# Half a piece in each tick, in place of a whole piece in every other one, for chains that stand alone

## The chip, the cores and the metric

The kernel runs on one core of one Trainium2 chip. Its time is the device time in microseconds (us), the median of several runs; a profiled execution of the same program gives the trace.

## The reference

Two layers of cross attention, with x of shape (4, 1024, 512) and ctx of the same shape, all in fp32:

```python
def layer0(q, k, v):                       # 16 heads of 32
    Q, K, V = (heads(a @ W.T + b) for ...) # from x, ctx, ctx
    att = softmax(Q @ K.T / sqrt(32))
    x = (att @ V) @ Wo.T + bo + q
    return layernorm(x) * gamma + beta

def layer1(query, key, value):             # linear attention, no heads
    KV = einsum('bnd,bne->bde', elu(key), value)
    Z = 1 / (elu(query) . elu(key).sum(1) + 1e-6)
    x = query + (elu(query) @ KV) * Z
    return layernorm(x) * gamma + beta

x = layer0(x, ctx, ctx); x = layer1(x, ctx, ctx)
```

(`heads` and `layernorm` stand for what the reference writes out. The kernel works with elu(x) as the larger of x and exp(min(x, 0)) - 1.)

## The kernel before, in words

The work of layer 0 is cut into 64 units: 4 batches x 4 groups of 4 heads x 4 chunks of 256 queries. A unit has 16 half steps, so there are HALVES = 1024 of them, and the whole kernel is one loop over **ticks** k, from -14 to some 1,098, which every engine's program goes through in the same order. In tick k TensorE does, in this order:

- `pass1(k)`, line 471: one score matmul in two-term precision (512 keys for 128 queries of one head), into one of three banks `score`. VectorE takes its maximum (line 810).
- `pass2(k - 26)`, line 485: two matmuls of 256 columns into one of two banks `scoreT`, the maxima included. ScalarE takes the exponential into a ring `p_ring` of 7 places (line 657); GpSimd adds pairs of the ring (lines 1072, 1081), VectorE the other half of the sums (line 850), for the softmax's denominators.
- `beside(k)`: one **piece** of a chain, if the planner put one at this tick (`pieces[k]`).
- in every eighth tick (39, 47, 55, ...) a **visit**, lines 503 and 519: the product of four ring places with V. A tick with a visit never has a piece.

The **chains** are all other work of TensorE, and each accumulates in one of two banks `misc`, taken by turns. K (4 pieces of one fp32 matmul of 512 columns; line 542), V (4 pieces of 4 fp32 matmuls of 128 columns; 553) and Q (2 pieces of 2 matmuls of 256 columns; 529) are projections; O (4 pieces of 512 columns; 565) is the output projection of a tile of 128 rows; T (573) turns a tile's features, and A (4 pieces; 582) multiplies them with the key-value sum of layer 1; S (8 pieces of 512 columns; 590) makes that sum from features that ScalarE (746, 749) and VectorE (990) make some ticks ahead and GpSimd sums up (1123, 1127); N totals the features; B folds a bias. An fp32 matmul is two instructions on TensorE, each with a weight load of its own; fp32r matmuls (score, scoreT, A) are one.

When a chain's last piece has ended, ScalarE and VectorE take the result out of the bank in the same tick, by `ended`, and the next chain but one waits for that in `chain_freed`. `follow` then books the steps behind it: transfers on SP's queue by `send`, norms on ScalarE, VectorE and GpSimd by `book`, each at the first tick with room.

The planner walks through the ticks. At each tick without a visit it takes, of the chains that are ready, the one whose due time (`deadline`) comes first, and lays its pieces into the ticks that follow. A chain is **alone** by this test:

```python
alone = len(able) == 1 and 0 <= k < HALVES and (k < UT * UB or k % (UT * UB) >= 180) and deadline(*chain) - k > 2 * LENGTH[chain[0]] + 4
```

UT * UB is 256, the ticks of a batch. A chain that is alone has its pieces in every other tick: after each piece (`k - 1 in pieces`) one tick stays free. All other chains have theirs in tick after tick.

`sum_piece(k)` tells ScalarE, VectorE and GpSimd which feature to make for the S piece at tick k; they ask for it with k + 4, k + 3 and k + 2. The ring `fphi_sb` has 3 places; VectorE waits in `context_features` for `T["kv_piece"]` of the piece three before.

The tail: after tick 1023 there are no more scores, after tick 1049 no second passes, and the last batch's eight tiles go through O, norm, T, A and the last norm.

Of the kernel before, what the change touches and what calls it, by code (L numbers as in the profile page):

```python
# [12 lines left out]
def build(nc, x, xT, ctx, ctxT, WqT, WkT, WvT, cols, WoT, bo, gamma0, beta0, gamma1, beta1, out):  # L13
    B, S, D = x.shape
    P = nc.NUM_PARTITIONS
# [58 lines left out]
    with ExitStack() as c:  # L74
# [122 lines left out]

        LENGTH = {"K": 4, "V": 4, "Q": 2, "O": 4, "T": 1, "A": 4, "S": 8, "N": 1, "B": 4}  # L200
        TILE_TICKS = 21

# [124 lines left out]
        def follow(kind, i):  # L327
# [28 lines left out]
            if kind == "S":  # L356
                if i % G == G - 1 and i < G * (B - 1):
                    for t in range(0, KT, 2):
                        send("ctx", end + 2 + t, KT * (i // G + 1) + t, 2)
                for k in range(start_of["S", i], end + 1):  # L360
                    if k in pieces and pieces[k][0] == ("S", i):
                        take("ACT", k - 4, 5)
                        take("DVE", k - 3, 5)
                        take("POOL", k - 2, 5)
            elif kind == "O":
                k = finish_norm(i, 0, end)
                k = book("below", "ACT", max(k + 2, dot_of.get(i - 2, FIRST) + 1), 7, i)
# [15 lines left out]
        while waiting:  # L383
# [34 lines left out]
        LAST = max(store_of.values()) + 2  # L418
        assert all(tiles == sorted(tiles) for tiles in
# [16 lines left out]
        def bank_of(kind, i):  # L436
            return misc[number[kind, i] % 2]
# [10 lines left out]

        def sum_piece(k):

            chain, piece = pieces.get(k, (None, 0))
            return KT * chain[1] + piece if chain and chain[0] == "S" else None


        def tensor_program():
# [68 lines left out]
            def q_project(unit, piece):  # L524
                if piece == 0:
# [5 lines left out]
                if piece == 1:  # L531
                    mm.then_inc(T["q_projected"], 1)

            def k_project(i, t):
                group, h = divmod(i, 2)
                if t == 0:
                    pe.wait_ge(M["wk"], landed(group, 1, 1))
                if i == 0:
                    pe.wait_ge(M[f"ctxT_block{t}"], 16)
                elif t == 0 and (h > 0 or group >= G):  # L540
# [5 lines left out]
            def v_project(i, t):  # L546
                group, h = divmod(i, 2)
                if t == 0:
# [6 lines left out]
                if t == G - 1:  # L555
                    mm.then_inc(T["v_projected"], 1)

            def o_project(tile, g):
                b, t = divmod(tile, KT)
                unit = unit_at[G * b + g, t // TPC]  # L560
                if g == 0:
# [3 lines left out]
                mm = pe.matmul(bank_of("O", tile)[:], outT[:, unit % NO, t % TPC * P:(t % TPC + 1) * P], wo[:, g, :],  # L565
                               start=g == 0, stop=g == G - 1)
                if g == G - 1:
                    mm.then_inc(T["o_projected"], 1)

            def turn_phi(tile):  # L570
# [13 lines left out]
                if d == G - 1:  # L584
                    mm.then_inc(T["attended"], 1)

            def sum_kv(i, t):
                piece = KT * i + t
                pe.wait_ge(V["f_phi"], piece + 1)
                pe.matmul(bank_of("S", i)[:], fphi_sb[:, piece % NPHI, :], ctx_nat[:, t, :],  # L590
                          start=t == 0, stop=t == KT - 1).then_inc(T["kv_piece"], 1)

            def total(b):
                pe.wait_ge(L["totalled"], G * (KT - 1) * (b + 1))
# [9 lines left out]
                    mm.then_inc(T["bias_passed"], 1)  # L604

            def beside(k):
                chain, piece = pieces.get(k, (None, 0))
                if not chain:
                    return
                kind, i = chain  # L610
                if piece == 0 and chain_freed(kind, i):
                    pe.wait_ge(*chain_freed(kind, i))
                if kind == "Q":
                    q_project(i, piece)
                elif kind == "K":
                    k_project(i, piece)
                elif kind == "V":
                    v_project(i, piece)
                elif kind == "O":
                    o_project(i, piece)  # L620
                elif kind == "T":
                    turn_phi(i)
                elif kind == "A":
                    attend(i, piece)
                elif kind == "S":
                    sum_kv(i, piece)
# [723 lines left out]
```

## Time and profile before

| what | us |
|---|---|
| median of 3 runs | 1512.66 (1512.58 to 1513.71) |
| span of the profiled execution | 1509.6 |
| own time of the profiled execution | not given apart from its span |
| TensorE busy | 1473.3 |
| VectorE busy | 1227.3 |
| GpSimd busy | 1206.0 |
| ScalarE busy | 900.9 |
| TensorE weight loads busy | 1038.6 |

The span runs from the first instruction to the last; a run's time holds what lies around it too. PE is TensorE, PEld its weight loads, DVE VectorE, ACT ScalarE, POOL GpSimd, SP SyncE. A matmul's recorded duration takes in the pipeline, so the sums of PE overlap; the time that one takes of the engine is seen in the distance from start to start. A matmul's record can begin while the one before it still streams.

### The profile page before, as it was taken

What the parts mean: (1) busy time and instruction counts of PE and PEld (TensorE: products, weight loads), DVE (VectorE), ACT (ScalarE), POOL (GpSimd) and SP (SyncE); (2) the same over time, 40 slices, a digit from 0 to 9 for tenths busy, and PEclk for the clock granted to TensorE, in tenths of its full rate; (3) what the DMA queues carried; (4) which work ended last, traced back from release to release, by engine and by line L of the source; (5) the groups of instructions that cost most, each with busy time, mean ns of one, the idle gap of its engine ahead of it and who ended that gap; (6) DMA issues with size and microseconds to landing.
All of it is one profiled execution on the core that took longest, in us unless ns stands there. A gap on an engine that the chain in (4) does not pass through costs nothing.

```text
span 1509.6 us, 30353 instructions
## 1 busy us (share of the span) xinstructions
PE 1473.3 (98%) x10584; PEld 1038.6 (69%) x10584; DVE 1227.3 (81%) x2442; ACT 900.9 (60%) x1846; POOL 1206.0 (80%) x1031
## 2 busy tenths in 40 slices
PE   8999999999999999999999999999999999999996
PEld 6767767676766767667677767766767767766554
DVE  6687898878788788887779788898688978899865
ACT  3464655556666666665566665665566666566664
POOL 0487787867898898877789988887789888888964
PEclk9999999999999999999999999999999999999999
DMA  7745163443425225344343425424252442520001
GB/s 222 200 144 143 54 181 128 130 128 97 122 73 157 89 90 146 105 132 138 90 129 98 135 68 158 149 87 133 79 157 77 129 127 70 148 88 26 14 23 42
DMA packets 159575, 170.14 MB, mean 113 GB/s; under 512 B 20288, under 2 KB 122048, under 8 KB 159424
## 3 DMA queue, kind: packets, MB, share of 16 engines
q1 hardware_dynamic: 157696, 167.16, 37.4%
q8 instruction: 84, 1.38, 0.4%
q10 hardware_dynamic: 1728, 1.05, 0.2%
q14 instruction: 67, 0.55, 0.1%
HBM read 125.97 MB, written 42.21 MB: 111 GB/s over the span
## 4 chain that ended last, share of the span: by engine, by line
PE 85%; DVE 4%; DMA 3%; issue 3%; POOL 2%; ACT 2%; SPq 1%; POOLq 0%; ACTq 0%; DVEq 0%
PE score L471 15%; PE scoreT L485 14%; PE acc L503 14%; PE misc L565 7%; PE misc L542 7%; PE misc L553 7%; PE misc L590 7%; PE misc L529 6%; PE misc L582 5%; PE acc L519 2%; DVE maxes L810 1%; POOL pair_sum L1072 1%; DMA q_stack<-q_dram 1%; PE misc L573 1%; DVE pair_sum L850 1%
## 5 line engine op out<-in xcount | busy, mean ns | idle before, releaser
L657 ACT ACTIVATE p_ring<-scoreT 128x512 f32<-128x512 f32 x1024 | 594.2, 594 | 496.9 <-PE scoreT L485 493.6
L1072 POOL TENSOR_TENSOR pair_sum<-p_ring 128x512 f32<-128x512 f32 x504 | 665.5, 1329 | 173.9 <-ACT p_ring L657 111.5
L810 DVE TENSOR_REDUCE maxes<-score 128x1 f32<-128x512 f32 x1024 | 677.3, 679 | 151.2 <-PE score L471 146.0
L471 PE MATMUL score<-k_stack,q_stack 96*128 96x512 f32 x1024 | 599.5, 587 | 5.4 <-DVE maxes L810 2.1
L485 PEld LDWEIGHTS scoreT<-q_stack,k_stack 104*128 104x128 f32 x2048 | 387.7, 191 | 156.7 <-ACT p_ring L657 81.6
L485 PE MATMUL scoreT<-q_stack,k_stack 104*128 104x256 f32 x2048 | 419.7, 287 | 7.3 <-ACT p_ring L657 5.1
L471 PEld LDWEIGHTS score<-k_stack,q_stack 96*128 96x128 f32 x1024 | 193.1, 189 | 161.5 <-issue 106.6
L503 PE MATMUL acc<-p_ring,v_sb 128*32 128x256 f32 x4096 | 249.9, 385 | 0.0
L1081 POOL TENSOR_TENSOR pair_sum<-pair_sum 128x512 f32<-128x512 f32 x189 | 248.8, 1316 | 0.0
L850 DVE TENSOR_TENSOR pair_sum<-pair_sum 128x512 f32<-128x512 f32 x189 | 197.2, 1043 | 1.9 <-POOL pair_sum L1072 1.7
L503 PEld LDWEIGHTS acc<-p_ring,v_sb 128*32 128x32 f32 x4096 | 120.6, 110 | 85.3 <-issue 3.2
L553 PE MATMUL misc<-wv,ctxT_sb 128*128 128x128 f32 x1024 | 134.6, 274 | 0.0
L565 PE MATMUL misc<-wo,outT 128*128 128x512 f32 x256 | 131.1, 599 | 3.4 <-DVE ctxT_sb L966 2.7
L542 PE MATMUL misc<-ctxT_sb,wk 128*128 128x512 f32 x256 | 131.1, 596 | 1.6 <-DMA ctxT_sb<-ctxT_in 1.6
L590 PE MATMUL misc<-ctx_nat,fphi_sb 128*128 128x512 f32 x256 | 132.0, 596 | 0.5 <-DVE fphi_sb L990 0.5
L529 PE MATMUL misc<-xT_sb,wq 128*128 128x256 f32 x512 | 131.6, 379 | 0.2 <-DVE k_low L903 0.2
L553 PEld LDWEIGHTS misc<-wv,ctxT_sb 128*128 128x128 f32 x1024 | 126.0, 191 | 0.8 <-issue 0.5
L1101 POOL TENSOR_TENSOR tiles<-tiles,gamma_row 128x512 f32<-128x512 f32 x52 | 72.2, 1389 | 34.8 <-ACT tiles L693 34.7
L529 PEld LDWEIGHTS misc<-xT_sb,wq 128*128 128x128 f32 x512 | 88.4, 189 | 8.6 <-issue 0.7
L990 DVE SCALAR_TENSOR_TENSOR fphi_sb<-f_sb,ctx_nat 128x128 f32<-128x128 f32 x128 | 81.7, 638 | 1.6 <-ACT f_sb L749 1.3
L1093 POOL TENSOR_TENSOR rstd<-var_eps,minus_half 128x1 f32<-128x1 f32 x64 | 40.3, 630 | 40.9 <-ACT var_eps L704 40.5
L1127 POOL TENSOR_TENSOR phi_total<-phi_total,fphi_sb 128x128 f32<-128x128 f32 x96 | 54.4, 567 | 23.1 <-DVE fphi_sb L990 22.8
(112 smaller groups left out, 1373.9 us busy)
## 6 DMA issues: line engine op xcount, KB each, us to landing
xT_sb<-xT_in SPq DMA_DIRECT2D x63, 512.0 KB, 3.8
q_stack<-q_dram SPq DMA_DIRECT2D x189, 128.0 KB, 2.6
k_stack<-k_dram SPq DMA_DIRECT2D x93, 256.0 KB, 4.7
ctx_nat<-ctx_in SPq DMA_DIRECT2D x32, 256.0 KB, 4.7
q_dram<-q_high SPq DMA_DIRECT2D x63, 128.0 KB, 1.9
q_dram<-q_low SPq DMA_DIRECT2D x63, 128.0 KB, 2.1
k_dram<-k_high SPq DMA_DIRECT2D x31, 256.0 KB, 2.0
k_dram<-k_low SPq DMA_DIRECT2D x31, 256.0 KB, 2.2
```

Source lines behind the costliest of these rows:

```text
L471: pe.matmul(score[k % 3][:], q_stack[0:SPLIT, unit % NQ, j, t * P:(t + 1) * P], k_stack[0:SPLIT, group_of[unit] % 2 * QUAD + j, h * HALF:( ...
L485: mm = pe.matmul(scoreT[k % 2][:, (j % 2) * CH:(j % 2 + 1) * CH], k_stack[0:ROWS, group_of[unit] % 2 * QUAD + j, kt * P:(kt + 1) * P], q_s ...
L503: mm = pe.matmul(acc[j * DK:(j + 1) * DK, 0:CH], v_sb[:, group % 2, kt, j * DK:(j + 1) * DK], p_ring[:, n % NP, j * CH:(j + 1) * CH], star ...
L529: mm = pe.matmul(bank_of("Q", unit)[:, 0:CH], wq[:, t, :], xT_sb[:, unit % 2, t, :], start=t == 0, stop=t == G - 1)
L542: mm = pe.matmul(bank_of("K", i)[:], wk[:, t, :], ctxT_sb[:, h, t, :], start=t == 0, stop=t == G - 1)
L553: mm = pe.matmul(bank_of("V", i)[:, t * P:(t + 1) * P], ctxT_sb[:, h, f, t * P:(t + 1) * P], wv[:, f, :], start=f == 0, stop=f == G - 1)
L565: mm = pe.matmul(bank_of("O", tile)[:], outT[:, unit % NO, t % TPC * P:(t % TPC + 1) * P], wo[:, g, :], start=g == 0, stop=g == G - 1)
L590: pe.matmul(bank_of("S", i)[:], fphi_sb[:, piece % NPHI, :], ctx_nat[:, t, :], start=t == 0, stop=t == KT - 1).then_inc(T["kv_piece"], 1)
L657: act.activation(p_ring[:, n % NP, h * HALF:(h + 1) * HALF], scoreT[k % 2][:], ACT.Exp, scale=SCALE).then_inc(A["exped"], 1)
L810: dve.reduce_max(maxes[:, unit % 2, t, j, h:h + 1], score[k % 3][:], AX.X).then_inc(V["maxed"], 1)
L1072: pool.tensor_tensor(pair_sum[:, place_of_pair(pair), cols], p_ring[:, (n - 1) % NP, cols], p_ring[:, n % NP, cols], ALU.add).then_inc(L[" ...
L1081: pool.tensor_tensor(whole, whole, part, ALU.add).then_inc(L["run_low"], 1)
```

## The change

Chains of the kinds K, V, Q, O and S that are alone are now `halved`: each piece is two parts, FIRST_PART and SECOND_PART, in the next two ticks that have no visit, with no tick left free after them. K, O and S pieces are halved by columns (`columns_of`: 256 of 512 for each part, with the same weights loaded for both), V and Q pieces by source blocks (`steps_of`: the same matmuls, the first half of them in the first part). Waits at a chain's or a piece's start are in the first part, increments in the second. Of the chains that are alone, only others (A, T, N, B) keep the free ticks. A feature of an S piece is made and booked by its first part's tick.

```diff
+        WHOLE, FIRST_PART, SECOND_PART = range(3)
...
-                    if k in pieces and pieces[k][0] == ("S", i):
+                    if k in pieces and pieces[k][0] == ("S", i) and pieces[k][2] != SECOND_PART:
                         take("ACT", k - 4, 5)
                         take("DVE", k - 3, 5)
                         take("POOL", k - 2, 5)
...
+            halved = alone and chain[0] in "KVQOS"
             for piece in range(LENGTH[chain[0]]):
-                if alone and k - 1 in pieces:
+                if alone and not halved and k - 1 in pieces:
                     k += 1
-                while visiting(k) is not None:
+                for part in (FIRST_PART, SECOND_PART) if halved else (WHOLE,):
+                    while visiting(k) is not None:
+                        k += 1
+                    pieces[k] = chain, piece, part
+                    end_of[chain] = k
                     k += 1
-                pieces[k] = chain, piece
-                end_of[chain] = k
-                k += 1
...
-            chain, piece = pieces.get(k, (None, 0))
-            return KT * chain[1] + piece if chain and chain[0] == "S" else None
+            chain, piece, part = pieces.get(k, (None, 0, WHOLE))
+            return KT * chain[1] + piece if chain and chain[0] == "S" and part != SECOND_PART else None
+
+        def columns_of(part):
+
+            return {WHOLE: slice(0, HALF), FIRST_PART: slice(0, HALF // 2), SECOND_PART: slice(HALF // 2, HALF)}[part]
+
+        def steps_of(part, first, count):
+
+            middle = first + count // 2
+            return {WHOLE: range(first, first + count), FIRST_PART: range(first, middle),
+                    SECOND_PART: range(middle, first + count)}[part]
...
-                for t in range(2 * piece, 2 * piece + 2):
+                for t in steps_of(part, 2 * piece, 2):
...
-                mm = pe.matmul(bank_of("K", i)[:], wk[:, t, :], ctxT_sb[:, h, t, :], start=t == 0, stop=t == G - 1)
-                if t == G - 1:
+                mm = pe.matmul(bank_of("K", i)[:, columns_of(part)], wk[:, t, :], ctxT_sb[:, h, t, columns_of(part)],
+                               start=t == 0 and part != SECOND_PART,
+                               stop=t == G - 1, skip_group_check=True)
+                if t == G - 1 and part != FIRST_PART:
                     mm.then_inc(T["k_projected"], 1)
...
-                for f in range(G):
+                for f in steps_of(part, 0, G):
...
-                pe.wait_ge(V["f_phi"], piece + 1)
-                pe.matmul(bank_of("S", i)[:], fphi_sb[:, piece % NPHI, :], ctx_nat[:, t, :],
-                          start=t == 0, stop=t == KT - 1).then_inc(T["kv_piece"], 1)
+                if part != SECOND_PART:
+                    pe.wait_ge(V["f_phi"], piece + 1)
+                mm = pe.matmul(bank_of("S", i)[:, columns_of(part)], fphi_sb[:, piece % NPHI, :],
+                               ctx_nat[:, t, columns_of(part)], start=t == 0 and part != SECOND_PART,
+                               stop=t == KT - 1, skip_group_check=True)
+                if part != FIRST_PART:
+                    mm.then_inc(T["kv_piece"], 1)
```

O pieces are changed as K's are, and all functions take the part as one more argument.

## Rows read from the trace of the kernel before

**Rows 1.** The page, parts 1, 2 and 5: busy us (share of the span), instructions; slices; groups.

```profile
PE 1473.3 (98%) x10584; PEld 1038.6 (69%) x10584; DVE 1227.3 (81%) x2442; ACT 900.9 (60%) x1846; POOL 1206.0 (80%) x1031
...
PE   8999999999999999999999999999999999999996
...
PEclk9999999999999999999999999999999999999999
...
L1072 POOL TENSOR_TENSOR pair_sum<-p_ring 128x512 f32<-128x512 f32 x504 | 665.5, 1329 | 173.9 <-ACT p_ring L657 111.5
L810 DVE TENSOR_REDUCE maxes<-score 128x1 f32<-128x512 f32 x1024 | 677.3, 679 | 151.2 <-PE score L471 146.0
```

**Rows 2.** Timeline of TensorE around 75 us: start, us, what, xcount [idle before].

```profile
75.17 0.40 PE L471 MATMUL score<-k_stack,q_stack 96*128 96x512 f32 x1
...
75.64 0.39 PE L471 MATMUL score<-k_stack,q_stack 96*128 96x512 f32 x1
77.64 0.51 PE L485 MATMUL scoreT<-q_stack,k_stack 104*128 104x256 f32 x2 [1.61 <-ACT p_ring L657]
77.98 0.39 PE L471 MATMUL score<-k_stack,q_stack 96*128 96x512 f32 x1
...
80.94 0.63 PE L471 MATMUL score<-k_stack,q_stack 96*128 96x512 f32 x1
```

**Rows 3.** Timeline of TensorE, 206 to 213 us: K pieces, then Q pieces, in consecutive ticks.

```profile
206.54 0.79 PE L471 MATMUL score<-k_stack,q_stack 96*128 96x512 f32 x1
...
207.87 0.80 PE L471 MATMUL score<-k_stack,q_stack 96*128 96x512 f32 x1
...
210.75 0.59 PE L471 MATMUL score<-k_stack,q_stack 96*128 96x512 f32 x1
...
212.09 0.58 PE L471 MATMUL score<-k_stack,q_stack 96*128 96x512 f32 x1
```

**Rows 4.** Timeline of TensorE, 115 to 118 us: a K chain with empty ticks between.

```profile
115.66 0.40 PE L471 MATMUL score<-k_stack,q_stack 96*128 96x512 f32 x1
...
116.13 1.02 PE L542 MATMUL misc<-ctxT_sb,wk 128*128 128x512 f32 x2
116.59 0.80 PE L471 MATMUL score<-k_stack,q_stack 96*128 96x512 f32 x1
...
117.46 0.40 PE L471 MATMUL score<-k_stack,q_stack 96*128 96x512 f32 x1
...
118.39 0.80 PE L471 MATMUL score<-k_stack,q_stack 96*128 96x512 f32 x1
```

**Rows 5.** Timeline of TensorE at 37 us, before the second pass begins.

```profile
37.13 0.50 PE L471 MATMUL score<-k_stack,q_stack 96*128 96x512 f32 x1 [0.18 <-DVE maxes L810]
```

**Rows 6.** Windows of core 0: PE, PEld, DVE, ACT, POOL busy (x), PEclk, DMA share, GB/s.

```profile
77.98:82.34 4.36, 4.36 (x15) 2.83 (x14) 3.94 (x12) 2.99 (x9) 3.28 (x4) 0.61 0.42 135
344.80:348.20 3.40, 3.36 (x22) 1.96 (x24) 3.25 (x5) 1.53 (x3) 3.40 (x4) 0.50 0.31 99
1339.00:1360.00 21.00, 20.46 (x142) 12.97 (x142) 21.00 (x37) 13.37 (x33) 20.77 (x20) 1.00 0.16 47
1460.00:1510.00 50.00, 36.05 (x242) 22.95 (x240) 24.19 (x63) 25.63 (x57) 20.96 (x21) 0.95 0.09 32
```

**Rows 7.** Window of line 590 alone (S 5): PE and PEld busy (x), PEclk, DMA share.

```profile
612.60:633.00 20.40, 8.22 (x16) 2.46 (x16) 1.00 0.19 60
```

**Rows 8.** Timeline of TensorE: V pieces in a row, V piece alone, Q piece alone.

```profile
47.23 0.48 PE L471 MATMUL score<-k_stack,q_stack 96*128 96x512 f32 x1
...
48.61 0.48 PE L471 MATMUL score<-k_stack,q_stack 96*128 96x512 f32 x1
...
55.31 0.40 PE L471 MATMUL score<-k_stack,q_stack 96*128 96x512 f32 x1
...
57.16 0.40 PE L471 MATMUL score<-k_stack,q_stack 96*128 96x512 f32 x1
...
67.23 0.40 PE L471 MATMUL score<-k_stack,q_stack 96*128 96x512 f32 x1
...
69.05 0.40 PE L471 MATMUL score<-k_stack,q_stack 96*128 96x512 f32 x1
```

More of the change, by code:

```diff
@@ L522, in visit, with q_project, k_project @@
                 mm.then_inc(T["divided"], 1)
-            def q_project(unit, piece):
-                if piece == 0:
+            def q_project(unit, piece, part):
+                if piece == 0 and part != SECOND_PART:
                     pe.wait_ge(M["wq"], 16 * (wq_load_of[unit] + 1))
                     pe.wait_ge(M[f"xT{unit % 2}"], landed(unit, 2, 1))
-                for t in range(2 * piece, 2 * piece + 2):
+                for t in steps_of(part, 2 * piece, 2):
                     mm = pe.matmul(bank_of("Q", unit)[:, 0:CH], wq[:, t, :], xT_sb[:, unit % 2, t, :],
                                    start=t == 0, stop=t == G - 1)
-                if piece == 1:
+                if piece == 1 and part != FIRST_PART:
                     mm.then_inc(T["q_projected"], 1)
-            def k_project(i, t):
+            def k_project(i, t, part):
                 group, h = divmod(i, 2)
-                if t == 0:
+                if t == 0 and part != SECOND_PART:
                     pe.wait_ge(M["wk"], landed(group, 1, 1))
@@ L539, in k_project, with v_project @@
                     pe.wait_ge(M[f"ctxT_block{t}"], 16)
-                elif t == 0 and (h > 0 or group >= G):
+                elif t == 0 and part != SECOND_PART and (h > 0 or group >= G):
                     pe.wait_ge(M[f"ctxT{h}"], ctxT_landed(group // G, h))
-                mm = pe.matmul(bank_of("K", i)[:], wk[:, t, :], ctxT_sb[:, h, t, :], start=t == 0, stop=t == G - 1)
-                if t == G - 1:
+                mm = pe.matmul(bank_of("K", i)[:, columns_of(part)], wk[:, t, :], ctxT_sb[:, h, t, columns_of(part)],
+                               start=t == 0 and part != SECOND_PART,
+                               stop=t == G - 1, skip_group_check=True)
+                if t == G - 1 and part != FIRST_PART:
                     mm.then_inc(T["k_projected"], 1)
-            def v_project(i, t):
+            def v_project(i, t, part):
                 group, h = divmod(i, 2)
-                if t == 0:
+                if t == 0 and part != SECOND_PART:
                     pe.wait_ge(M["wv"], landed(group, 1, 1))
@@ L551, in v_project, with o_project @@
                         pe.wait_ge(M[f"ctxT{h}"], ctxT_landed(group // G, h))
-                for f in range(G):
+                for f in steps_of(part, 0, G):
                     mm = pe.matmul(bank_of("V", i)[:, t * P:(t + 1) * P], ctxT_sb[:, h, f, t * P:(t + 1) * P],
                                    wv[:, f, :], start=f == 0, stop=f == G - 1)
-                if t == G - 1:
+                if t == G - 1 and part != FIRST_PART:
                     mm.then_inc(T["v_projected"], 1)
-            def o_project(tile, g):
+            def o_project(tile, g, part):
                 b, t = divmod(tile, KT)
                 unit = unit_at[G * b + g, t // TPC]
-                if g == 0:
+                if g == 0 and part != SECOND_PART:
                     pe.wait_ge(V["out_scaled"], unit_at[G * b + G - 1, t // TPC] + 1)
@@ L564, in o_project @@
                         pe.wait_ge(M["wo"], 16)
-                mm = pe.matmul(bank_of("O", tile)[:], outT[:, unit % NO, t % TPC * P:(t % TPC + 1) * P], wo[:, g, :],
-                               start=g == 0, stop=g == G - 1)
-                if g == G - 1:
+                mm = pe.matmul(bank_of("O", tile)[:, columns_of(part)], outT[:, unit % NO, t % TPC * P:(t % TPC + 1) * P],
+                               wo[:, g, columns_of(part)], start=g == 0 and part != SECOND_PART,
+                               stop=g == G - 1, skip_group_check=True)
+                if g == G - 1 and part != FIRST_PART:
                     mm.then_inc(T["o_projected"], 1)
@@ L585, in attend, with sum_kv @@
                     mm.then_inc(T["attended"], 1)
-            def sum_kv(i, t):
+            def sum_kv(i, t, part):
                 piece = KT * i + t
-                pe.wait_ge(V["f_phi"], piece + 1)
-                pe.matmul(bank_of("S", i)[:], fphi_sb[:, piece % NPHI, :], ctx_nat[:, t, :],
-                          start=t == 0, stop=t == KT - 1).then_inc(T["kv_piece"], 1)
+                if part != SECOND_PART:
[5 more added lines that the diff above has]
+                    mm.then_inc(T["kv_piece"], 1)
             def total(b):
@@ L606, in beside @@
             def beside(k):
-                chain, piece = pieces.get(k, (None, 0))
+                chain, piece, part = pieces.get(k, (None, 0, WHOLE))
                 if not chain:
@@ L610, in beside @@
                 kind, i = chain
-                if piece == 0 and chain_freed(kind, i):
+                if piece == 0 and part != SECOND_PART and chain_freed(kind, i):
                     pe.wait_ge(*chain_freed(kind, i))
                 if kind == "Q":
-                    q_project(i, piece)
+                    q_project(i, piece, part)
                 elif kind == "K":
-                    k_project(i, piece)
+                    k_project(i, piece, part)
                 elif kind == "V":
-                    v_project(i, piece)
+                    v_project(i, piece, part)
                 elif kind == "O":
-                    o_project(i, piece)
+                    o_project(i, piece, part)
                 elif kind == "T":
@@ L625, in beside @@
                 elif kind == "S":
-                    sum_kv(i, piece)
+                    sum_kv(i, piece, part)
                 elif kind == "N":
```

## The prediction

> **What bounds the kernel now.** I first read the page's busy times and slices [rows 1]. TensorE has work recorded for 98% of the span, VectorE for 81%, GpSimd for 80%; the two largest groups off TensorE, the maxima and the pair sums, take 677 and 666 us of 1510. But a busy TensorE is no proof that it is the bound, because a record there holds the pipeline's time too. So I went to the timeline of TensorE and measured from one score matmul to the next, which is one tick.
>
> Two bare ticks, with no piece in them, give the price of the fixed work: from 75.17 to 75.64, 0.47 us [rows 2]. Four ticks in a row that each hold a K piece cost 1.33 us each; one pair of such starts is shown (206.54 to 207.87) [rows 3]. So a K piece costs 1.33 - 0.47 = 0.86 us. S and O pieces are the same two 512-column instructions, and the ticks in a row with them that I looked at read 1.33 too.
>
> Now the stretch that the change is about. A lone K chain has a piece in every other tick. From 115.66 over 116.59, 117.46 to 118.39 the starts alternate by 0.93 and 0.87 [rows 4]. The late share is only a matter of recording: the score's record begins while the piece before it still streams (piece at 116.13, score at 116.59, 0.46 later, for 0.86 us of work). The pair is 1.80 us (116.59 to 118.39), and 0.47 + 1.33 = 1.80. That is the main reading: in a lone chain a light and a heavy tick together take exactly TensorE's own work, with nothing left over. The three score banks and two scoreT banks already let VectorE and ScalarE average over a pair. I looked at 35 such pairs; 33 lie between 1.797 and 1.816 us by the starts of their score matmuls. There is no wait in them that an even spread could take away.
>
> Where does TensorE wait then? In clusters of ticks with nothing at all, such as 75.64 to 77.64, where scoreT waited 1.61 us for an exponential [rows 2]; at the start, where maxima alone pace the ticks [rows 5]; and in the last 50 us, where TensorE has 36.05 us recorded of 50 [rows 6].
>
> **The change part by part.**
>
> *Who is halved.* Going through the planner as it stands, the test for a lone chain holds for 29 of the chains in K, V, Q, O, S: 8 S chains (0, 1, 3, 5, 6, 9, 10, 14) of 8 pieces, 5 K chains (2, 4, 5, 6, 8) and 4 V chains (1, 3, 7, 9) of 4, O 0 of 4, and 11 Q chains of 2. That is 64 + 20 + 4 = 88 pieces that are halved by columns, and 16 V and 22 Q pieces halved by source blocks. The trace bears the spacing out: S 5 needs 20.4 us for its 16 instructions [rows 7], where eight heavy ticks in a row would need 10.6 plus the visits between. All but eight of the 29 start before tick 250, so the change touches the first 335 us and three short stretches later. A few chains may gain or lose the property as the order moves.
>
> *Halving by columns (K, S, O).* Two instructions of 512 columns become four of 256: 176 matmuls and 176 weight loads more. The nearest row is a Q piece, which is just that, four fp32 instructions of 256 columns, each with its load. A tick with it costs 1.34 (210.75 to 212.09) against 1.33 [rows 3], and a bare tick and a Q tick 1.82 (67.23 to 69.05) against 1.80 [rows 4, 8]. So the finer cut costs 0.01 to 0.02 us a piece, the loads being hidden behind the columns of the instruction before. Halving also adds one more change from scoreT to piece and back to score in each pair. No row shows half a piece; from the Q rows, whose surplus holds one such change, a second costs from 0.00 to 0.02. Together 0.01 to 0.04 a piece; I take 0.02, nearer the Q piece amid others. Of the 88 I drop K 2's 4, in ticks that VectorE paces (score waits for a maximum at 37.13 [rows 5]), and S 14's 8, where VectorE is busy for 21.00 us of 21 and GpSimd for 20.77 [rows 6]. 76 x 0.02 = 1.5 us; bounds 0.8 and 3.0. If that cover were gone, the 12 would add 0.2.
>
> The Trainium skill's page "TensorE: Matmul & The Clock Gate", section "Back-to-back issue gap", gives a matmul at the high clock its columns at 2.4 GHz and 2.5 ns on top. By it, an estimate, two instructions more add 5 ns a piece and 0.4 us in all, instead of 1.5; it speaks for the low end.
>
> *Halving by blocks (V, Q).* Instructions keep their number and shape. V ticks in a row cost 1.38 (47.23 to 48.61), a bare and a V tick 1.85 (55.31 to 57.16) [rows 8], which is 0.47 + 1.38: nothing to gain, and one more change of kind costs 0 by V's rows. For Q I take 0.01 x 20 = 0.2 us (two of the 22 pieces lie in the paced start); bounds 0 and 0.4.
>
> *The waits.* First parts hold all waits of a chain's start, second parts the increments. So kv_piece comes one tick later. VectorE makes features three ticks ahead and waits for the piece three before: with pieces two ticks apart that one's second half lies five ticks behind the PE's score of the same number, so nobody waits: 0. Behind that feature on VectorE would stand the maxima, and behind them the scores; if the cover went, each of the 64 would show a gap. Evictions of K, Q, V, O, S are still tied to the chain's last half.
>
> *The order that moves.* A spaced chain of L pieces takes 2L - 1 ticks when it starts fresh, and a tick of visit costs it nothing when it falls on its empty tick. Halved, it takes 2L and steps over each visit. By hand: S 0 ends at tick 69 instead of 66, S 5 at 465 instead of 462, S 14 at 977 instead of 974, K 4 at 88 instead of 86, O 0 at 254 instead of 252. What follows starts later by as much, also its DMA issues on SP's queue (puts and stacks of keys and queries) and its bookings on ScalarE, VectorE and GpSimd. The planner calls a chain lone only if it has over 2L + 4 ticks to its due time, and the earliest ticks of the next chains take the shift up again (Q 7 at 74, K 4 at 80). TensorE's total work is the same. Where it is saturated, order alone costs 0. I take 0, with bounds from the rivals below.
>
> **The sum.** 1.5 + 0.2 = 1.7 us on a span of 1509.6. The page gives the profiled execution its span only; the median of the runs shown is 1512.66, 3.1 us above, and I put the gain or loss on that: 1512.66 + 1.7 = 1514.4, 0.11% slower. What a measurement here can tell from no change is 0.2%, 3.0 us: 1509.6 to 1515.7 counts as the same.
>
> **The rivals.**
>
> *The light clusters fill up: faster.* After a cluster the granted clock drops: 344.80 to 348.20 has it at 0.50, the 1.2 GHz level, after bare ticks [rows 6], 77.98 to 82.34 has a mean of 0.61 [rows 6], and there the ticks from 77.98 to 80.94 take 2.96 us instead of 1.80, behind the stall before them [rows 2]. If halves moved into two clusters, each would give back its stall, 1.61, and up to half of 3.4 us, 1.7: 2 x 3.3 = 6.6, less 1.7, so 1507.8. For it: chains end later, so gaps shrink by one to three ticks. Against it: the cluster at 75 gets only half a Q piece into tick 49, the stall ends when an exponential ends wherever the piece stands, and O 0's late end makes Q 18 start at tick 256, where the test forbids halving. It decides from two clusters on. Chance 0.12. The Trainium skill, on the same page ("TensorE: Matmul & The Clock Gate"), section "HAM oscillation — how this bites in real kernels", holds that gaps in TensorE's work bring the low clock back; by that rule the time would be this rival's, and the trace agrees that a drop follows a cluster but not that lone chains cause one.
>
> *The tail starts late: slower.* S 14 ends three ticks later; S 15, O 24 and O 25 queue behind it, and the last eight tiles' norms, turns and products hang on O 24. From 1460 on TensorE is no longer full [rows 6], so a delay isn't absorbed. Price: three heavy ticks, 3 x 1.33 = 4.0, plus 1.7: 1518.4. For it: the tail is a chain. Against it: between S 14 and there lie a dozen bare ticks, and VectorE and GpSimd are full from 1339 on, so GpSimd's own sum of work may set the end whatever O 24 does. It decides when O 24's product is over 1.5 us later. Chance 0.30.
>
> *The halves do not spread anything.* If order shifts undo more than the halves add (chains lose the lone property), the cost is some 0.5 us: 1513.2; inside the forecast's case.
>
> **How the numbers follow.** Forecast's case 0.53, its own range 1512.5 to 1516.5 (bounds 0.8 and 3.4 and an odd stall); faster rival 0.12; slower 0.30; 0.05 for the unforeseen, split evenly. The forecast's case reaches over 1515.7 in a small part, 0.03, and the slower rival, half paid, falls below it in 0.06. So faster 0.14, same 0.55, slower 0.31. The range is 1510.0 to 1519.0: it holds the forecast's case, part of the faster one and nearly all of the slower.
>
> **What would show it.** Right: TensorE ticks in lone S, K, O chains of 0.90 to 0.92 us each, evenly; a pair within 0.02 to 0.04 of 1.80; 10760 matmuls; no new wait of VectorE's features. Wrong: halves that take over 0.45 us each (loads not hidden), which would add up to several us; a clock without its drops near 79 and 345 us; or O 24's pieces ending more than 2 us after 1387 and the end following them.

## The result and the profile after

The changed kernel takes 1522.63 us (median of 6 runs, 1519.71 to 1527.48) against 1513.49 for the kernel before on the same chips: a ratio of 1.0067, with an interval of 1.005 to 1.0084. It is slower by about 9 to 10 us. The forecast was 1514.4, with a range up to 1519.0.

The page of the changed kernel, parts 1, 2 and 5, answers to [rows 1]:

```profile
span 1524.8 us, 30625 instructions
...
PE 1483.7 (97%) x10720; PEld 1068.9 (70%) x10720; DVE 1229.1 (81%) x2442; ACT 903.5 (59%) x1846; POOL 1203.4 (79%) x1031
...
PEclk9999999999999999999999999999999999999998
...
L830 DVE TENSOR_REDUCE maxes<-score 128x1 f32<-128x512 f32 x1024 | 676.6, 678 | 153.4 <-PE score L484 150.3
...
L607 PE MATMUL misc<-ctx_nat,fphi_sb 128*128 128x256 f32 (+1 forms) x352 | 139.8, 477 | 2.3 <-DVE fphi_sb L1010 2.3
```

TensorE has 136 instructions more (10720 against 10584), so 68 pieces were cut by columns, not 88. The profiled execution is the slowest of the six: its span is 1524.8 us, its time 1527.48. The span is 15.2 above that of before; 9 of these are what the medians show too.

The timeline of TensorE in the lone chain S 5 (line 484 is the score, 498 scoreT, 607 the S piece) answers to [rows 4]:

```profile
614.77 0.58 PE L484 MATMUL score<-k_stack,q_stack 96*128 96x512 f32 x1
...
615.43 0.60 PE L607 MATMUL misc<-ctx_nat,fphi_sb 128*128 128x256 f32 x2
615.68 0.58 PE L484 MATMUL score<-k_stack,q_stack 96*128 96x512 f32 x1
...
616.34 0.60 PE L607 MATMUL misc<-ctx_nat,fphi_sb 128*128 128x256 f32 x2
616.58 0.58 PE L484 MATMUL score<-k_stack,q_stack 96*128 96x512 f32 x1
```

Each tick now holds half a piece and they are even, 0.91 and 0.90 us from score to score. Two of them, 614.77 to 616.58, take 1.81 us where the pair of before took 1.80. Cutting the pieces costs next to nothing and gives nothing. The loss must be elsewhere.

**Where it is.** I took the start of the score matmul of each tick in both traces, and from the difference I took away the work that one plan had put ahead of that tick and the other not yet (0.86 us for a K, S, O or N piece, 0.87 for Q, 0.90 for V, 0.72 for A, 0.63 for T, as the ticks in a row have them). What is left is time truly lost or won since the start:

```
changed kernel against before, us lost, by tick
tick     144   256   440   464   512   528   592   704   720   768   800   960   976    end
lost     0.3   0.6   0.5   1.5   1.6   2.2   2.5   2.8   3.8   3.8   5.5   6.0   7.2   15.2
```

Between the steps the curve is flat to a few hundredths of a microsecond; from tick 272 to 440, where both plans are the same, it doesn't move at all. So the list of steps is short: 1.1 us in S 5 (448 to 464) and 1.0 in S 9 (704 to 720); where the plan behind these two differs, 1.2 from 512 to 704 and 1.7 from 768 to 800; 0.5 from 800 to 960, most of which traces with before's plan show too; 1.2 in S 14 (960 to 976); and 8 us after tick 976. This last number is not a safe one. The kernels below that keep before's tail move by -1.5 (e10) to +3.1 us (e2) after tick 976, and this execution has TensorE at the 1.2 GHz level for 28 us there, before's for 11.

The planner shows what differs behind S 5. Halved, S 5 ends at tick 465, not 462, and K 16 at 472, not 469. Before, at tick 470, S 6 was the only chain that could start (K 17 may from tick 472 on), so it went next and alone. Now, at 473, both can, and K 17 is due earlier. S 6 comes at 480, with V 16 ready beside it, so that it isn't alone any more and goes whole, in ticks in a row:

```profile
656.64 0.80 PE L484 MATMUL score<-k_stack,q_stack 96*128 96x512 f32 x1
...
657.98 0.80 PE L484 MATMUL score<-k_stack,q_stack 96*128 96x512 f32 x1
```

V 16 and V 17 come sooner than before too, and new clusters of bare ticks open up later on: 517, 518, 520 and 521, where the curve loses 0.6 us, and, behind the same turn at S 9 and S 10, 773, 774, 782, 789 and 790, where it loses 1.7. (The bare ticks at 580 to 584 are as many as before, there at 581 to 585.) In such a cluster TensorE outruns the other engines and waits. Here are the bare ticks 789 and 790 and what follows up to the score of tick 792; scoreT waits twice for an exponential and a score once for a maximum:

```profile
1097.97 0.39 PE L484 MATMUL score<-k_stack,q_stack 96*128 96x512 f32 x1
1098.60 0.50 PE L498 MATMUL scoreT<-q_stack,k_stack 104*128 104x256 f32 x2 [0.24 <-ACT p_ring L677]
1099.31 0.50 PE L484 MATMUL score<-k_stack,q_stack 96*128 96x512 f32 x1 [0.21 <-DVE maxes L830]
1100.10 0.50 PE L498 MATMUL scoreT<-q_stack,k_stack 104*128 104x256 f32 x2 [0.28 <-ACT p_ring L677]
...
1102.39 0.50 PE L484 MATMUL score<-k_stack,q_stack 96*128 96x512 f32 x1
```

Windows of core 0, with the columns of [rows 6], for the same places:

```profile
344.80:348.20 3.40, 3.40 (x27) 1.82 (x29) 3.40 (x6) 1.88 (x4) 3.40 (x3) 0.73 0.10 22
1350.60:1371.70 21.10, 19.44 (x152) 14.21 (x148) 20.50 (x37) 12.15 (x28) 20.50 (x21) 1.00 0.15 47
1474.00:1524.00 50.00, 34.54 (x209) 22.06 (x201) 24.41 (x56) 19.41 (x43) 17.74 (x18) 0.83 0.08 31
```

The stretch of S 14 looks as it did, with VectorE and GpSimd nearly full. The clock between 344.80 and 348.20 is 0.73 as a mean, where it was 0.50. The last row is for 50 us near the end: TensorE is busy for less and has a clock of 0.83, where before had 36.05 us and 0.95 [rows 6].

### The profile page after: what moved, and what is told of

It reads as the page before. It is cut to its first block, busy times and chain, and to the rows that moved or that the text cites. A ratio compares the mean times of both kernels' runs of the same rounds, so it can differ in the third digit from the quotient of the medians.

```text
span 1524.8 us, 30625 instructions
## 1 busy us (share of the span) xinstructions
PE 1483.7 (97%) x10720; PEld 1068.9 (70%) x10720; DVE 1229.1 (81%) x2442; ACT 903.5 (59%) x1846; POOL 1203.4 (79%) x1031
## 4 chain that ended last, share of the span: by engine, by line
PE 78%; POOL 7%; DVE 6%; issue 5%; DMA 2%; ACT 2%; SPq 1%; POOLq 0%; ACTq 0%; DVEq 0%
PE score L484 14%; PE acc L516 13%; PE scoreT L498 13%; PE misc L555 7%; PE misc L568 6%; PE misc L542 6%; PE misc L607 6%; PE misc L580 5%; PE misc L598 5%; POOL pair_sum L1092 3%; DVE maxes L830 2%; PE acc L532 2%; DVE pair_sum L870 1%; POOL pair_sum L1101 1%; DVE fphi_sb L1010 1%
## 5 line engine op out<-in xcount | busy, mean ns | idle before, releaser
L677 ACT ACTIVATE p_ring<-scoreT 128x512 f32<-128x512 f32 x1024 | 602.1, 593 | 515.5 <-PE scoreT L498 507.6
L607 PE MATMUL misc<-ctx_nat,fphi_sb 128*128 128x256 f32 (+1 forms) x352 | 139.8, 477 | 2.3 <-DVE fphi_sb L1010 2.3
L542 PE MATMUL misc<-xT_sb,wq 128*128 128x256 f32 x512 | 136.2, 381 | 1.4 <-DMA xT_sb<-xT_in 1.2
L555 PE MATMUL misc<-ctxT_sb,wk 128*128 128x512 f32 (+1 forms) x288 | 134.8, 552 | 1.9 <-DMA ctxT_sb<-ctxT_in 1.8
L580 PE MATMUL misc<-wo,outT 128*128 128x512 f32 (+1 forms) x264 | 130.8, 580 | 2.2 <-DVE ctxT_sb L986 1.7
```

Source lines behind the costliest of these rows:

```text
L555: mm = pe.matmul(bank_of("K", i)[:, columns_of(part)], wk[:, t, :], ctxT_sb[:, h, t, columns_of(part)], start=t == 0 and part != SECOND_PA ...
L607: mm = pe.matmul(bank_of("S", i)[:, columns_of(part)], fphi_sb[:, piece % NPHI, :], ctx_nat[:, t, columns_of(part)], start=t == 0 and part ...
L677: act.activation(p_ring[:, n % NP, h * HALF:(h + 1) * HALF], scoreT[k % 2][:], ACT.Exp, scale=SCALE).then_inc(A["exped"], 1)
```

## The experiments

The changed kernel's plan is before's from tick 258 to 442 and again from 791 to 960, so the parts of the change can be tried apart: in the first batch, in the two middle ones, and in the last. Each line has a median, the median of before measured beside it, and the ratio with its interval. The ratio isn't the quotient of the two medians: it is up to 0.14 percentage points away from it (e3: 1.0055, the quotient 1.0041), so differences of about 1 us between two lines say nothing.

```
run                     us        before    ratio   interval
e1_first_batch          1510.48   1512.58   0.9987  0.9976 to 0.9998
e2_middle               1516.67   1512.58   1.0035  1.0020 to 1.0050
e3_last_batch           1518.80   1512.58   1.0055  1.0038 to 1.0071
e4_last_held            1513.85   1512.58   1.0017  1.0005 to 1.0028
e5_middle_whole         1518.73   1513.27   1.0037  1.0022 to 1.0051
e6_first_whole          1511.78   1513.27   0.9991  0.9980 to 1.0003
e7_held_lead            1512.17   1513.27   0.9990  0.9977 to 1.0003
e8_no_s                 1513.65   1513.27   1.0001  0.9987 to 1.0015
e9_tail_order           1513.56   1513.03   1.0011  0.9996 to 1.0026
e10_middle_lead         1514.95   1513.03   1.0013  0.9998 to 1.0028
e11_first_again         1511.42   1513.03   0.9983  0.9969 to 0.9998
e12_all_tail_order      1515.15   1512.45   1.0012  1.0001 to 1.0023
```

### One batch at a time

```diff
-            halved = alone and chain[0] in "KVQOS"
+            halved = alone and chain[0] in "KVQOS" and k < UT * UB                        # e1
+            halved = alone and chain[0] in "KVQOS" and UT * UB <= k < 3 * UT * UB         # e2
+            halved = alone and chain[0] in "KVQOS" and k >= 3 * UT * UB                   # e3
```

> Halves only for chains that start before tick 256; later lone chains keep the free ticks, and the plan from tick 264 on is the one of before. By the order theory (a halved tick costs TensorE what the pair did, and the loss comes where the order of later chains changes): same as before, +0.5 us (-1 to +2), since the traces stand 0.45 us apart from tick 264 to 440. By the theory of my prediction (each halved piece costs 0.02 us): +1 us. By a theory that halving itself is what costs: most of the 9 us, at least +5 us, as 76 pieces of some 98 are halved here.

> Halves only in the second and third batch (Q 30, S 5, Q 46, S 9: 20 pieces). Order theory: +4 to +6 us, with the two losses of the trace after the change (ticks 456 to 640 and 712 to 800), because S 6 and S 10 are no longer alone and go whole behind K and Q. Theory that halving itself costs: under +2 us, since only 20 pieces are halved.

> Halves only in the last batch: S 14 and, since it is alone now, Q 63; the planner then puts O 24 and O 25 ahead of S 15. Order theory: +2 to +8 us, all of it after tick 960. Theory that the tail follows from work, not order (VectorE and GpSimd full): within 1 us of before.

76 pieces halved in the first batch make the kernel faster, by 2.1 us; 20 in the middle cost 4.1 us, 10 in the last 6.2. The three ratios together (-0.13, +0.35 and +0.55%) come to +0.77%, the changed kernel has +0.67%. A cost of each halved piece as the cause of the loss is out, for the loss goes against the number of pieces. (Whether a piece costs my 0.02 us or nothing these runs can't tell; the rows of S 5 above can.)

### The order of the tail

```diff
+        HELD = dict(entry.split(":") for entry in (
+            "217:S14* 218:Q63 219:S15 220:O24 221:O25 222:N3* ").split())
...
+            held = HELD.get(str(len(chains)))
+            if held:
+                able = [chain for chain in able if chain == (held[0], int(held[1:].rstrip("*")))]
```

At each number of chains already placed, only the chain named may come next; a star keeps it alone.

> As the one before, S 14 halved, but the planner must take Q 63, S 15, O 24, O 25 and N 3 in the order of the kernel before, so that O 24 ends three ticks later and everything from T 24 on has its old ticks. If the new order of the tail is the loss: within 1 us of before. If three ticks of delay of O 24 are (the rival of my prediction): +3 to +4 us, as much as the one before.

e4 is at +1.3 us, with S 14 halved and O 24 ending three ticks later, at 993. By the same reckoning as above it loses 1.2 us between ticks 960 and 976, in S 14, and then nothing more to the end (2.6 at 976, 2.6 at the end). Its ratio, 1.0017, would leave room for more than that step, but e7 below has the same delay and is not slower than before (0.9990). So a delay of three ticks costs the tail little or nothing. The planner's new order does cost, e3's interval lying above e4's. In it O 24 and O 25 go ahead of S 15, which looks like a gain: in e3 O 24's first matmul is at 1373.84 us, where before it was at 1381.82. But later T 29 and A 29 go ahead of O 30 and O 31. e9 undoes that swap alone:

```diff
+        HELD = dict(entry.split(":") for entry in (
+            "236:A28 237:O30 238:O31 239:T29 240:A29 241:T30 242:T31 243:A30 244:A31 ").split())
```

> The plan of e3_last_batch until T 28; the last nine chains in the order of the kernel before, with O 30 and O 31 ahead of T 29 and A 29. In e3_last_batch O 31 started 5.1 us later than before, behind A 29, and A 31 8.6 us later. If that swap is the loss of the tail: the time falls from +6.2 us to +1 to +3 us. If the loss is made earlier (O 24 and O 25 ahead of S 15, N 3 and A 24 later): still +5 us or more.

The last 30 us of TensorE in before (565 is O, here O 30 and O 31 together, 573 is T, 582 is A), then in e3 (580, 589, 598), in e4 and in e9 (both 585, 594, 603):

```profile
1480.49 7.03 PE L565 MATMUL misc<-wo,outT 128*128 128x512 f32 x16
1487.35 0.60 PE L573 MATMUL misc<-ident,e_sb 128*128 128x128 f32 x4
...
1495.61 0.63 PE L573 MATMUL misc<-ident,e_sb 128*128 128x128 f32 x4 [2.10 <-DVE e_sb L945]
...
1501.33 0.39 PE L582 MATMUL misc<-kv_high,k_low 128*128 128x512 f32 x1
```

```profile
1485.31 0.39 PE L598 MATMUL misc<-kv_high,k_low 128*128 128x512 f32 x1
1485.54 7.03 PE L580 MATMUL misc<-wo,outT 128*128 128x512 f32 x16
1497.58 1.09 PE L589 MATMUL misc<-ident,e_sb 128*128 128x128 f32 x4 [5.02 <-DVE e_sb L965]
...
1501.12 0.63 PE L598 MATMUL misc<-kv_high,phiT_low 128*128 128x512 f32 x1
1501.55 0.63 PE L598 MATMUL misc<-kv_high,phiT_high 128*128 128x512 f32 x1
...
1510.06 0.39 PE L598 MATMUL misc<-kv_high,k_low 128*128 128x512 f32 x1
```

```profile
1483.13 7.03 PE L585 MATMUL misc<-wo,outT 128*128 128x512 f32 x16
...
1498.23 0.63 PE L594 MATMUL misc<-ident,e_sb 128*128 128x128 f32 x4 [2.10 <-DVE e_sb L970]
...
1503.93 0.39 PE L603 MATMUL misc<-kv_high,k_low 128*128 128x512 f32 x1
```

```profile
1477.97 7.10 PE L585 MATMUL misc<-wo,outT 128*128 128x512 f32 x16 [1.48 <-DVE outT L900]
1484.92 0.60 PE L594 MATMUL misc<-ident,e_sb 128*128 128x128 f32 x4
...
1493.46 0.63 PE L594 MATMUL misc<-ident,e_sb 128*128 128x128 f32 x4 [2.98 <-DVE e_sb L970]
...
1500.79 0.39 PE L603 MATMUL misc<-kv_high,k_low 128*128 128x512 f32 x1
```

In e3 A 29's last matmul is at 1485.31 and O 30 comes right behind it, at 1485.54. Its features are then wanted while nothing is left to do: T 30 waits 5.02 us for them, and from O 30's first matmul to A 31's last pass 24.5 us (1485.54 to 1510.06). In before the same way takes 20.8 us (1480.49 to 1501.33), because T 29 and A 29 lie in the gap, at 1487.35 to 1492.67. Part of the 24.5 us is the clock. Windows of core 0 for e3 and e9:

```profile
1495.20:1505.40 10.20, 6.36 (x17) 4.76 (x18) 6.47 (x17) 4.11 (x8) 0.75 (x1) 0.50 0.07 26
1494.70:1498.10 3.40, 3.40 (x10) 2.63 (x9) 0.69 (x1) 0.80 (x2) 2.56 (x2) 0.50 0.02 5
```

From 1495.2, within its wait, to 1505.4 e3 is at the 1.2 GHz level (the clock column reads 0.50). Eleven starts of A 30's matmuls take 4.7 us there (0.43 each) instead of 2.5 (0.23 each), so at least 2.2 of the 3.7 us that e3 is longer than before came that way; before isn't at the low level until 1505.3.

With O 30 and O 31 ahead again, e9 needs 22.8 us, about 1.6 of them from its own shorter low stretch, and starts the two chains at 1477.97. Its time is +0.5 us, a ratio of 1.0011 against e3's 1.0055. e12 has the whole change with this tail:

> The whole change, but the last nine chains in the order of the kernel before (O 30 and O 31 ahead of T 29 and A 29). If the parts add up as the separate runs had them (first batch -2 us, middle +4 to +5, last batch with this order +0.5 to +1.7): +3 to +4.5 us against before, that is 4 to 6 us less than the changed kernel. If the tail's swap only mattered by itself: still +8 us or so.

It comes to +2.7 us, ratio 1.0012, a little less than I expected and 0.55 percentage points below the whole change. So the swap of two pairs of chains is the larger part of what the change lost.

### The middle: the plan, or the halves?

```diff
-                if not chain:
+                if not chain or part == SECOND_PART:    # all pieces whole, in the first part's tick
                     return
+                part = WHOLE
```

> The plan of e2_middle tick for tick, but each halved piece goes whole in its first part's tick, and the second part's tick stays bare. If the plan's order is the loss in the middle, as much slower as e2_middle (+4 us, at least +2.5). If cutting pieces in two is the loss: as before.

> The plan of e1_first_batch, with whole pieces in the first part's tick. If the 2 us that e1_first_batch gained come from the order and the filled ticks of its plan: also -1 to -2 us. If they come from the even spread of work: as before, within 1 us.

e5 has the plan of e2 and no halves, and is as slow: 1.0037 and 1.0035. Its steps are also those of e2 and of the changed kernel: 1.0 us from tick 448 to 464, 0.6 to 528, 1.0 in S 9, 1.8 from 768 to 800. The plan is the loss. e6 has the plan of e1 and keeps about two thirds of its gain; its interval reaches 1.0003 and overlaps e1's, so how much the halves add isn't settled.

What S 5 loses is seen at its end. The timeline of TensorE in the changed kernel, and in e5:

```profile
626.71 0.50 PE L484 MATMUL score<-k_stack,q_stack 96*128 96x512 f32 x1
627.04 0.41 PE L498 MATMUL scoreT<-q_stack,k_stack 104*128 104x256 f32 x2
627.81 0.70 PE L607 MATMUL misc<-ctx_nat,fphi_sb 128*128 128x256 f32 x2 [0.36 <-DVE fphi_sb L1010]
628.41 0.50 PE L484 MATMUL score<-k_stack,q_stack 96*128 96x512 f32 x1
```

```profile
627.19 0.50 PE L484 MATMUL score<-k_stack,q_stack 96*128 96x512 f32 x1
627.53 0.40 PE L498 MATMUL scoreT<-q_stack,k_stack 104*128 104x256 f32 x2
628.29 1.13 PE L607 MATMUL misc<-ctx_nat,fphi_sb 128*128 128x512 f32 x2 [0.36 <-DVE fphi_sb L1011]
628.89 0.76 PE L484 MATMUL score<-k_stack,q_stack 96*128 96x512 f32 x1
```

Both wait 0.36 us for the same feature, recorded in front of the piece, and the next score comes late. Halved or not, the piece stands at tick 461, behind a visit that moved it from even to odd ticks; before it stood at 460 and didn't wait. S 9's piece at 717 and S 14's at 973, as far into their chains, wait 0.36 and 0.35 us in the changed kernel. I thought that VectorE makes this feature right behind its sum of pairs, which falls on every fourth tick, and that one tick more of lead would mend it:

```diff
+        def early_piece(k):
+
+            if pieces.get(k, (None, 0, WHOLE))[2] == WHOLE and sum_piece(k) is not None:
+                return sum_piece(k)
+            return sum_piece(k + 1) if pieces.get(k + 1, (None, 0, WHOLE))[2] == FIRST_PART else None
...
-                piece = sum_piece(k + 4)
+                piece = early_piece(k + 4)
```

VectorE's k + 3 is changed in the same way; e7 has this in e4, e10 in e2.

> e4_last_held, but ScalarE and VectorE make the features of S 14's halved pieces one tick earlier. Theory: the 1.2 us that ticks 960 to 976 lost in e4_last_held come because a feature, made three ticks ahead of its first part, falls behind VectorE's sum of pairs and the half piece waits for it; then the loss there falls below 0.4 us and the kernel comes to within 0.5 us of before. If VectorE and GpSimd are simply full there: no change, 1.2 us again.

> e2_middle with the features of S 5's and S 9's halved pieces made a tick earlier on ScalarE and VectorE. If the 1.0 us that the S 5 stretch loses (ticks 448 to 464), and S 9's, come from features behind VectorE's pair sum: about half of each comes back, as in e7_held_lead (1.2 fell to 0.7), and the rest of the trace keeps e2_middle's steps. Time +3 us. If not: the same two steps of 1.0 us, +4 us.

In e7 the loss in S 14 fell from 1.2 to 0.7 us, short of what I expected; in e10 the step in S 9 was 0.5 us instead of 1.5 in e2, but the step in S 5 stayed at 1.0. The traces say why. These are TensorE's waits for VectorE in the stretch of S 5 (us in total, times, longest; PEld is the weight load in front of a matmul, lines 484 and 490 are the score), in e2 (window 612 to 634), then in e10 (609 to 632):

```profile
PEld score L484 <- DVE maxes L830: 0.7, 2, 0.4
PEld misc L607 <- DVE fphi_sb L1010: 0.6, 1, 0.6
PE misc L607 <- DVE fphi_sb L1010: 0.4, 1, 0.4
```

```profile
PEld score L490 <- DVE maxes L836: 1.7, 5, 0.4
```

With a tick more of lead the wait for the feature is gone, and the scores wait longer for their maxima instead, which VectorE makes as well. It is the same in e7: neither piece of S 14 waits any more, but the score of tick 973 waits 1.18 us for a maximum, where in e4 it waited 0.53. So the early features only moved VectorE's delay from one of its products to the other. That VectorE is behind in these stretches is shown. Why it is behind is not. Just before S 5's piece waits, VectorE works without a gap from 624.28 to 627.76 us in the changed kernel, and its sum of pairs there takes longer than the one in before:

```profile
624.88 1.17 DVE L870 TENSOR_TENSOR pair_sum<-pair_sum 128x512 f32<-128x512 f32 x1
```

```profile
625.38 0.68 DVE L850 TENSOR_TENSOR pair_sum<-pair_sum 128x512 f32<-128x512 f32 x1
```

What makes the same operation take 1.17 us in one place and 0.68 in the other no run here separates.

The medians came down by more than those steps (e7 0.9990 against e4 1.0017, e10 1.0013 against e2 1.0035), which the trace doesn't account for and which I don't claim.

### Without S, and the first batch again

```diff
-            halved = alone and chain[0] in "KVQOS"
+            halved = alone and chain[0] in "KVQO"       # e8
```

> Only K, V, Q and O chains are halved, in all batches; S chains keep whole pieces in every other tick. The order of all chains from tick 443 on is that of before. If the loss needs the halved S chains (their three ticks more that turn the order): -1 to -3 us, like e1_first_batch. If every kind loses: slower than before.

> The kernel of e1_first_batch once more, on other runs. Order theory with the gain of the first run: 1 to 2 us below before. If that gain was chance: within 0.5 us of before.

e8 keeps before's order of chains from tick 443 on and isn't slower: the loss needs the halved S chains, whose three ticks more turn the order. It isn't faster either, other than I expected; it lacks the halves of S 0, S 1 and S 3, and the rows below show what that leaves in place. e11 repeats e1: 0.9983 after 0.9987, both with intervals below 1. It beats both kernels, by 1.6 to 2.1 us.

Where at least part of that gain lies can be seen. In e1, e11, e6 and the changed kernel 1.5 us come back from tick 64 to 80 and 1.1 us from 128 to 144; in e2, e3, e4, which have before's plan there, nothing does. (Some 0.9 of the 1.5 had been lost just before, from tick 60 to 64 in S 0; 0.7 fall on tick 80 alone.) The timeline of TensorE at the end of the first of these, before and in e11:

```profile
110.00 0.40 PE L471 MATMUL score<-k_stack,q_stack 96*128 96x512 f32 x1
110.38 0.50 PE L485 MATMUL scoreT<-q_stack,k_stack 104*128 104x256 f32 x2
...
113.75 0.50 PE L471 MATMUL score<-k_stack,q_stack 96*128 96x512 f32 x1 [0.53 <-DMA q_stack<-q_dram]
```

```profile
109.90 0.58 PE L484 MATMUL score<-k_stack,q_stack 96*128 96x512 f32 x1
110.32 0.40 PE L498 MATMUL scoreT<-q_stack,k_stack 104*128 104x256 f32 x2
...
112.94 0.50 PE L484 MATMUL score<-k_stack,q_stack 96*128 96x512 f32 x1
```

Before, two bare ticks (72, 73) and light ones let TensorE run ahead to the scores of unit 5 at tick 80, where it waits 0.53 us for the unit's queries to land in q_stack. In e11 the halves of S 0, Q 6 and Q 7 lie in those ticks, the queries are there in time, and tick 80 starts at 112.94 instead of 113.75. All 14 traces agree: the five with the new first batch (e1, e6, e11, e12 and the changed kernel) have no such wait at tick 80; the other nine wait from 0.53 (before) to 1.82 us. The longest is e8's, whose plan still leaves ticks 72 and 73 bare, S 0 being whole:

```profile
115.97 0.50 PE L484 MATMUL score<-k_stack,q_stack 96*128 96x512 f32 x1 [1.82 <-DMA q_stack<-q_dram]
```

So e8 keeps the largest wait that e1 is rid of, which fits its missing gain.

## Why the prediction was wrong

**The reading of the bound** was right. Pairs in lone chains held no wait (1.80 us), and the even spread gained nothing in them (1.81).

**Who is halved**: 26 chains, not 29, for K 8, Q 18, S 6 and S 10 lost the property and Q 63 got it. I said that a few might change and gave it no price. S 6 and S 10 are the ones around which the order turned. (The 20.4 us that I gave for S 5's instructions [rows 7] are the length of the window; its first piece starts at 613.18 us and its last ends at 628.94, which is 15.8 us. Nothing in the sum hangs on it.)

**Halving by columns**, 1.5 us by 0.02 a piece, was too high: 0.01 a piece by the S 5 rows, some 0.6 us for the 56 pieces outside K 2 and S 14. The rule of the Trainium skill ("TensorE: Matmul & The Clock Gate", section "Back-to-back issue gap"), which gave 5 ns a piece and 0.4 us, was nearer. **Halving by blocks** gave no loss that shows.

**The waits**: "nobody waits: 0" failed for three chains, S 5, S 9 and S 14. Their steps are 1.0 to 1.2 us each, 3.3 in all; 0.35 of each is a wait for a feature, most of the rest are scores that wait for maxima. For S 5 and S 9, e5 shows it for whole pieces too, so it isn't the later increment; the new plan puts the piece at a tick where VectorE is behind. Of S 5's 1.1 us not all need be the change's: where S 5 has before's plan, the same ticks lose between 0 and 0.7 us (0.7 in e9, where a score waits for a maximum). S 14's stretch has a feature wait of 0.54 us in before already, at tick 966.

**The order that moves** is the step that failed, in the words "TensorE's total work is the same. Where it is saturated, order alone costs 0. I take 0". TensorE is saturated only as long as the plan leaves it no cluster of bare ticks, and the order decides that: +0.35% in the middle with whole pieces as with halves (e5, e2). And in the tail it isn't saturated: +0.55% in e3, 0.11% with the last nine chains put back (e9). So order, put at 0, measured +4 to +5 us in the middle and +6 to +8 in the last batch (most of that by the swap), and about -2 in the first. The delays that I worked out were right, three ticks for S 5 and S 14 and two for O 0. That they would be taken up again held in the first batch, though not as I had it (Q 7 starts at 75, not 74, and N 0 goes ahead of K 8), and failed where they let another chain become ready in time to be chosen.

**The rival of the late tail** had the place right and the mechanism wrong. S 14 did end at 977, but e4 has that delay and its trace loses nothing after tick 976; O 24 wasn't late in the changed kernel but early (its first matmul is at 1377.75 us, before at 1381.82, though tick 976 starts 6.4 us later than before). **The rival of the filled clusters** was partly right, by e1 and e11, which gain 1.6 to 2.1 us. The part that the traces show came through a wait for queries, not through the clock: 12 of the 14 traces, those of e1 and e11 among them, have a stretch at the 1.2 GHz level near 77 us, near 345 us, or at both, and the two that have none, e3 and e9, have before's plan there. **The chances** don't quite add up by their own terms: these give faster 0.145, same 0.56 and slower 0.295, where I wrote 0.14, 0.55 and 0.31.

What stays open: what puts VectorE behind in S 5, S 9 and S 14, and how much of the changed kernel's profiled tail (8 us, where e3's has 3.7) is the low clock of that one execution. After tick 976 it is at the 1.2 GHz level for 28.1 us, e3 for 11.3 and e12, the same plan but for the last nine chains, for 10.8. By an estimate of mine from these, 17 us more at half the speed can cost up to 8 us where TensorE is busy, so the clock can account for the difference.

## What to carry to other kernels

A planner that takes, of what is ready, what is due first can turn a shift of a few ticks into another order: before a price is put on a change of pace, run the plan both ways and look for the places where the shift makes a second chain ready. An even spread inside a stretch was worth nothing here, where two or three buffers already average over it; look for the waits in the stretches with nothing in them, and at the end, where it paid to put the last two tiles' first step ahead of the remaining steps of the tile before them. A wait moved off one product of an engine that is behind can come back at another of its products (features and maxima here): read both before calling it mended. When the parts of a change can be put in one batch at a time, three runs do what no trace of the whole does.

## What the runs showed that I had not expected

Executions with the same plan differ in the first 195 us, by up to 1.1 us more up to tick 272, and then for a long time hardly any more. Against the trace of before, the loss at tick 144 is 0.4 (e2), 0.9 (e3), 0.4 (e4), 1.3 (e5), 1.2 (e7), -1.6 (e9) and -1.9 us (e10), all with before's plan there; from tick 272 to 432 none of these seven moves by more than 0.04 us. So differences of 3 us between single spans say nothing, and a step in the middle has to be set against what the same ticks do in the traces with before's plan. Those eight (e1, e3, e4, e6, e7, e8, e9, e11) read 0.1 to 0.9 us lost between ticks 448 and 960, up to 0.7 of it in S 5, and none of it between 768 and 800. That much of the 5.6 us that the changed kernel reads there need not be the change's.
